# Attention with experts: the last two expert products of a batch move into head 0 of the attention

## The reference, cut to what matters

```
qkv = x @ W_qkv + b_qkv                       # 16 heads of 16 channels
attn = softmax(q k^T / 4);  attn_out = attn @ v
gate = softmax(x @ W_gate + b_gate)           # 8 experts
top_g, top_i = top_k(gate, 2);  combine = one_hot(top_i) weighted by top_g
expert_out = x @ W_experts[e] + b_experts[e]  # all 8 experts
moe_out = sum_e expert_out[e] * combine[e]
out = layernorm(x + attn_out + moe_out)
```

## Time and profile before

| | us |
|---|---|
| median of 3 runs | 3752.07 |
| lowest and highest | 3751.63, 3758.32 |
| the profiled execution | 3751.49 |
| its span in the trace | 3749.7 |
| mean granted clock of PE over the span | 0.973 of 2.4 GHz |

### The profile page before, as it was taken

How to read it: one execution, slowest core, us unless ns; L and a number is a source line. 1 busy time by engine, 2 the same in 40 slices (tenths; PEclk the granted TensorE clock), 3 DMA queues, 4 the chain that set the end, 5 groups by cost and what they waited for, 6 DMA issues and landing times.

```text
span 3749.7 us, 119956 instructions
## 1 busy us (share of the span) xinstructions
PE 3492.4 (93%) x52122; PEld 1583.7 (42%) x52122; DVE 3251.9 (87%) x3105; ACT 2589.8 (69%) x3896; POOL 1785.5 (48%) x1565
## 2 busy tenths in 40 slices
PE   5999999999999989998599999999999999999997
PEld 3655555454555545555332423324233242332422
DVE  5899989989999998998589797997979979799796
ACT  3665757666575766655269497695976959769598
POOL 4787878878887887888031210312103121031210
PEclk7999999999999999999799999999999999999999
DMA  3443545444453444444340602406024060240600
GB/s 95 132 121 105 149 109 137 115 132 124 109 152 100 136 121 126 125 106 115 91 69 2 102 13 42 73 2 93 22 39 76 2 94 21 39 76 2 91 13 13
DMA packets 145233, 307.78 MB, mean 82 GB/s; under 512 B 24484, under 2 KB 64068, under 8 KB 144452
## 3 DMA queue, kind: packets, MB, share of 16 engines
q1 hardware_dynamic: 144708, 300.10, 35.2%
HBM read 230.68 MB, written 35.13 MB: 71 GB/s over the span
## 4 chain that ended last, share of the span: by engine, by line
PE 22%; ACT 10%; DVE 10%; issue 9%; DMA 0%; SPq 0%; ACTq 0%; DVEq 0%; POOL 0%
ACT probs L1532 10%; PE ps L1332 7%; PE ps L1319 6%; DVE neg_max L1640 3%; PE ps L1367 2%; PE ps L1280 2%; PE ps L1442 2%; PE ps L1347 1%; PE ps L1380 1%; DVE acc L1774 1%; DVE acc L1763 1%; DVE att L1684 1%; DVE x1T L1622 1%; DVE x1T L1620 1%; DVE acc L1766 0%
## 5 line engine op out<-in xcount | busy, mean ns | idle before, releaser
L350 POOL TENSOR_TENSOR z<-z,c_rep 128x1024 f32<-128x1024 f32 x512 | 1412.8, 2770 | 330.9 <-DVE z L867 322.3
L1532 ACT ACTIVATE probs<-ps,e_scale 128x512 f32<-128x512 f32 x2048 | 1242.5, 696 | 118.2 <-PE ps L1319 117.8
L867 DVE TENSOR_TENSOR_SCAN z<-dA,ps 128x1024 f32<-128x1024 f32 x512 | 1157.8, 2278 | 130.2 <-PE ps L408 82.2
L1640 DVE TENSOR_REDUCE neg_max<-ps 128x1 f32<-128x1024 f32 x1024 | 1191.8, 1218 | 58.9 <-PE ps L1280 57.5
L708 ACT ACTIVATE dA<-rep,a_rep 128x1024 f32<-128x1024 f32 x512 | 565.4, 1142 | 217.9 <-DVE z L867 214.4
L408 PEld LDWEIGHTS ps<-diag,u_t 64*64 64x64 f32 x32768 | 531.9, 135 | 389.1 <-issue 388.7
L1319 PE MATMUL ps<-q_st,k_st 50*128 50x512 f16 x2048 | 648.9, 389 | 26.6 <-ACT probs L1532 20.1
L1332 PE MATMUL ps<-probs,v_h 128*32 128x256 f32 x8192 | 657.2, 395 | 0.6 <-ACT o_sb L1539 0.6
L408 PE MATMUL ps<-diag,u_t 64*64 64x64 f32 x32768 | 599.0, 222 | 59.7 <-DVE z L867 40.5
L1280 PE MATMUL ps<-k_st,q_st 48*128 48x512 f16 x2048 | 614.0, 388 | 7.5 <-DVE neg_max L1640 6.6
L427 PE MATMUL ps<-z,eye 128*64 128x512 f32 x2048 | 506.1, 615 | 2.8 <-POOL z L350 2.3
(11 more groups left out here) (189 smaller groups left out, 3107.2 us busy)
## 6 DMA issues: line engine op xcount, KB each, us to landing
c_rep<-c_scratch SPq DMA_DIRECT2D x512, 256.0 KB, 4.0
rep<-delta SPq DMA_DIRECT2D x128, 256.0 KB, 4.5
q_st<-qk_halves SPq DMA_DIRECT2D x192, 128.0 KB, 10.0
k_st<-qk_halves SPq DMA_DIRECT2D x192, 128.0 KB, 10.5
qk_halves<-qk_parts SPq DMA_DIRECT2D x32, 512.0 KB, 10.6
x_nat<-in_x SPq DMA_DIRECT2D x9, 1024.0 KB, 7.9
x_rows<-x_nat SPq DMA_DIRECT2D x9, 1024.0 KB, 6.8
xT<-in_xT SPq DMA_DIRECT2D x8, 1024.0 KB, 7.5
```

Of the source, the lines that this page charges most:

```text
L350: pool.tensor_tensor(z[:, k % ZR, :], z[:, k % ZR, :], c_rep[:, slot, :], ALU.mult).then_inc(s_zc, 1)
L867: dve.tensor_tensor_scan(z[:, k % ZR, :], dA[:, k % AR, :], pair(1 + k % 2), 0.0, ALU.mult, ALU.add).then_inc(s_z, 1)
L1532: act.activation(probs[:, kt, half * HALF:(half + 1) * HALF], ps[:, ring_bank(("probs", h, 2 * kt + half)), :], ACT.Exp, scale=e_scale[:, ...
L1640: dve.tensor_reduce(neg_max[:, h % 2, qt:qt + 1], pair(qt % 2), AX.X, ALU.max, negate=True).then_inc(s_mx, 1)
```

## The change

The products u = 30 and 31, both of tile 7, leave `experts` and are done in head 0: u = 30 after the two `scores_t` of turn 0 and u = 31 after those of turn 2, both into bank 6, which `weigh_v` first uses in turn 4. The helper functions `expert`, `scale_expert` and `add_scaled` hold what was written in the loops. DVE adds u = 30 after the first maximum of head 2 (`add_last_expert`), ACT scales u = 31 after the seventh exponential, and POOL adds it after the copies for head 0. `join(b, 7)` moves on DVE from behind the first maximum of head 2 to behind the seventh. The banks 4 and 5 are freed for head 0 by the products 27 and 28 instead of 30 and 31. `scaled` moves from `probs` to the first half of `sq_e`, a tile that is used only in the setup, and ACT's wait for POOL in turn 2 of head 0 goes away. SP's program is the same.

```diff
+        scaled = sq_e[:, 0:4, :].rearrange("p (s e) n -> p s e n", s=2)
-        scaled = probs[:, 2, :].rearrange("p (s e n) -> p s e n", s=2, e=2)
...
-        EBANK = tuple((u + 4) % 8 if u < 8 else 4 + u % 3 for u in range(EU))
+        LAST = EU - 2
+        EBANK = tuple((u + 4) % 8 if u < 8 else 4 + u % 3 if u < LAST else 6 for u in range(EU))
...
+                for i in range(LAST // 2):
+                    add_scaled(i)
...
                     take_v_head(h, 0, 5)
                     take_v_head(h, 5, TT)
+                    if h == 0:
+                        add_scaled(LAST // 2)
...
             def ring_free(b, user):
...
                 if n == -3:
-                    used(b, EU - 2)
+                    used(b, LAST - 3)
                 elif n == -2:
-                    used(b, EU - 1)
+                    used(b, LAST - 2)
...
             def weigh_v(b, h, kt):
...
+                if h == 0 and kt == 0:
+                    used(b, EU - 1)
...
             def step(b, h, before, ahead, front):
...
+                    if h == 0 and kt in (0, 2):
+                        expert(b, LAST + kt // 2)
...
             def exp_unit(b, h, kt, half):
...
-                if h == 0 and kt == 2:
-                    act.wait_ge(s_pa, (b + 1) * EU + 4)
...
+            def scale_expert(b, u):
+
+                i = u // 2
+                act.wait_ge(s_ex, b * EU + (u + 1))
+                act.wait_ge(s_pa, b * EU + (2 * i + 2))
...
+                mul.then_inc(s_ec, 1)
...
             def step(b, h, before, turned):
...
                         exp_unit(b, h, kt, half)
+                        if h == 0 and kt == 3 and half == 0:
+                            scale_expert(b, EU - 1)
...
+            def add_last_expert(b):
+
+                i = b * (EU // 2) + LAST // 2
+                t, e = LAST // (E // 2), 2 * (LAST % (E // 2))
+                bank = ps[:, EBANK[LAST], :]
+                dve.wait_ge(s_ex, b * EU + (LAST + 1))
+                dve.wait_ge(s_ea, i)
+                dve.scalar_tensor_tensor(out=acc[:, t, :], in0=bank[:, 0:H], scalar=comb_s[:, t, e:e + 1],
+                                         in1=acc[:, t, :], op0=ALU.mult, op1=ALU.add).then_inc(s_es, 1)
+                dve.wait_ge(s_es, i + 1)
+                dve.scalar_tensor_tensor(out=acc[:, t, :], in0=bank[:, H:2 * H], scalar=comb_s[:, t, e + 1:e + 2],
+                                         in1=acc[:, t, :], op0=ALU.mult, op1=ALU.add).then_inc(s_ea, 1)
...
             def step(b, h, before):
...
                     take_max(b, h + PRE, qt)
                     if qt == 0 and not before:
+                        add_last_expert(b)
+                    if qt == 6 and not before:
                         join(b, TT - 1)
```

More of the change, by code:

```diff
@@ L1243, in _, with add_scaled @@
             for b in range(NB):
-                for i in range(EU // 2):
+                def add_scaled(i):
                     to = x_in[:, i // 2, :]
@@ L1425, in used, with expert @@
                 pe.wait_ge(s_ec if u % 2 else s_ea, b * (EU // 2) + (u // 2 + 1))
+            def expert(b, u):
+                t, e2 = u // (E // 2), u % (E // 2)
+                if EPREV[u] is not None:
+                    used(b, EPREV[u])
+                for i, (k, w, x) in enumerate(TERMS):
+                    mm = pe.matmul(ps[:, EBANK[u], :], x1T[:, x, k, t * P:(t + 1) * P],
+                                   w_e[:, w, k, e2 * 2 * H:(e2 + 1) * 2 * H], start=(i == 0), stop=(i == len(TERMS) - 1))
+                mm.then_inc(s_ex, 1)
             def experts(b):
@@ L1432, in experts @@
                         u = t * (E // 2) + e2
-                        if EPREV[u] is not None:
-                            used(b, EPREV[u])
+                        if u >= LAST:
+                            break
                         if u == 3:
@@ L1440, in experts @@
                             pe.wait_ge(s_we, 2 * e2 + 2)
[L1441 to L1444, removed]
+                        expert(b, u)
                         if u in EARLY:
@@ L1545, in take_max @@
                 act.activation(m_rows[:, :], ps[0:2 * TT, ring_bank(("rows", h, 0)), 0:P], ACT.Copy).then_inc(s_mr, 1)
+            def scale_expert(b, u):
+                i = u // 2
+                act.wait_ge(s_ex, b * EU + (u + 1))
+                act.wait_ge(s_pa, b * EU + (2 * i + 2))
+                for e in range(2):
+                    mul = act.activation(scaled[:, i % 2, e, :], ps[:, EBANK[u], e * H:(e + 1) * H], ACT.Copy,
+                                         scale=comb_s[:, u // 4, 2 * (u % 4) + e:2 * (u % 4) + e + 1])
+                mul.then_inc(s_ec, 1)
             def step(b, h, before, turned):
@@ L1584, in experts @@
                 act.wait_ge(s_cbs, b + 1)
[L1585 to L1592, removed]
+                for u in range(1, LAST, 2):
+                    scale_expert(b, u)
                     if u == 7:
```

## The result

| | before | changed |
|---|---|---|
| median of 5 runs, us | 3751.63 | 3796.0 |
| lowest and highest | 3749.89, 3758.32 | 3790.59, 3801.64 |
| span of the profiled execution | 3749.7 | 3794.2 |

The ratio is 1.0117, with a 95% interval of 1.0102 to 1.0131: slower by 1.2%. 3786 was forecast, with 3768 to 3800 as the range.

The account below looks back on a forecast made before the run. No single engine was taken to bound the changed stage; PE, DVE and ACT hand over by turns. Late rows +21, half clock +13, eighth batch -0.9, summed as +33.5 on 3751.5 plus 0.6: 3786 us, range 3768 to 3800.

Parts of the forecast that it names:

- The late `join` holding SP's queue: Last join behind six more maxima, SP's load behind it, head 1's rows behind the load: +21 us in all.
- The time of the load: Second batch: load of x_in issued at 2167.05 instead of 2159.82, 7.2 us later.
- The additional waits in head 0: Between DVE's six maxima of head 2: 0.4 us for the fourth's scores, 0.8 for the fifth's.
- The landing behind the load: Head 1's row copies arrive only with the load ahead of them, so PE starts head 1 at 2172.25.
- X + 5.2: X is the load's issue; upper bound for the rows' arrival, taking the load's 5.2 us.
- the rival of the passing rows: Head 1's rows pass the load, X + 4.25 or sooner: 3779 or 3776 us; chance 0.12.
- My reason for the bound: The 1024 KB load, 0.4 us ahead, occupies all DMA engines nearly the whole time; copies are 1 KB each.
- The clock behind the stall: After PE's 5.6 us standstill, head 1 starts at half clock: 1.9 us a batch, times seven, +13 us.
- the forecast's own range: 3774 to 3797: clock term between 7 x 1.3 - 1 and 7 x 2.5, join 0.7 us sooner or later.
- the faster rival: Load and rows arrive in time for head 1, so head 0's gains stand: 15 us, 3737; chance 0.06.
- The gain in head 0: Earlier banks: head 0 alone shorter by 2.4 us in second batch, 0.9 in fifth and eighth; clock expected at 1.00.

Follow-up runs that it names:

- Experiments 1 and 3: 1: changed kernel, SP issues head 1's row copies before join wait and load, 3731.26 us; 3: kernel before, last join behind head 2's seventh maximum, 3804.48 us.
- Experiment 2: Changed kernel, with SP issuing head 1's row copies behind its wait for the joins but ahead of the load: 3776.85 us, ratio 1.0069.
- Experiment 9: Changed kernel, with four extra 128-row matmuls per batch among the experts, behind the scores that follow u = 18: 3797.87 us, ratio 1.0113.
- experiment 5: Kernel before, with one extra 128-row, 512-column matmul behind each of head 0's first four turns, result unread: 3732.7 us, ratio 0.9948.

## Why the prediction was right

**The late `join` holding SP's queue: right.** Experiments 1 and 3 show it from both sides: with SP's order mended the loss is gone, and with the `join` alone moved it is there.

**The time of the load: right.** 11.8 us from the end of u = 28's addition was worked out and 11.45 measured. The additional waits in head 0 were put at 0.4 and 0.8 us and are 0.20 and 1.03.

**The landing behind the load: right in kind, too small.** I took X + 5.2; in the second batch head 1 started at X + 5.74 (2173.63 - 2167.89), and over the seven it was X + 5.74 to X + 6.20, 5.96 in the mean. The longest was the third, whose load left at 2409.94:

```profile
2416.14 0.60 PE L1325 MATMUL ps<-q_st,k_st 50*128 50x512 f16 x1 [6.22 <-DMA q_st<-m_rows]
```

Experiment 2 shows that the place behind the load costs the copies 1.8 us, so the rival of the passing rows fell. My reason for the bound, that the load occupies the DMA engines for nearly the whole time, was too strong. In the second batch they are busy for 3.4 us, from 1.1 us behind the load's issue on, and then nearly idle for 1.2 us until PE starts:

```profile
2169.00:2172.40 3.40, 0.00 (x0) 0.00 (x0) 0.00 (x0) 0.00 (x0) 0.80 (x4) 0.63 0.91 305
2172.40:2173.60 1.20, 0.00 (x0) 0.00 (x0) 0.00 (x0) 0.00 (x0) 0.00 (x0) 0.50 0.04 9
```

The Trainium skill says in "DMA: Bandwidth & Descriptors", section "Queues, rings and completion order", that each DMA engine takes descriptors in ring order, and these times fit that. The same section says that a later descriptor may finish its write before an earlier one, so the rule gives an order of starting and no landing time; the prediction drew more from it than it holds. Whether the copies are late by that order or because they share the busy engines with the load, no run separates.

**The clock behind the stall: right in kind, too small.** It was put at 1.9 us for each batch. From 2173.63 to about 2180.1 head 1 ran at half clock, 6.5 us, of which 37% is 2.4 us.

**No half clock among the experts: the term that was missing.** In before one batch had it behind u = 18. In the changed kernel seven have it, right behind PE's pause of 1.92 us there, and each costs 1.4 us (experiment 2). The pause and what follows, in the changed kernel:

```profile
2135.18 4.45 PE L1443 MATMUL ps<-w_e,x1T 128*128 128x512 f16 x12 [1.92 <-DVE acc L1812]
```

Experiment 9 puts work of 128 rows in that pause, and the spell is gone, but this doesn't show that the pause makes it. The first experiment has the same pause in the same batch, with the same code there, and no spell:

```profile
2125.00:2145.00 20.00, 17.98 (x89) 7.02 (x88) 19.61 (x33) 11.77 (x26) 9.01 (x16) 1.00 0.93 107
...
2135.05 2.76 PE L1444 MATMUL ps<-w_e,x1T 128*128 128x512 f16 x12 [1.91 <-DVE acc L1813]
```

PE is busy for 17.98 of 20 us in this window, as in that of the changed kernel in experiment 9. Why the spell comes in seven batches of the one and in none of the other is not settled. The distance from one batch to the next differs between the kernels, and that is the only difference I know of there; experiment 9 changes that distance too.

**All together.** Two neighbouring loads are (3137.18 - 2167.89) / 4 = 242.3 us apart after and (3099.36 - 2159.82) / 4 = 234.9 before, so 7.4 us for each batch, where my terms gave 4.9:

```profile
3137.18 0.38 SPq L1140 DMA_DIRECT2D x_in<-x_rows  x1
```

From the end of u = 28's second addition to the start of head 1 it was 13.9 us before and is 17.4 now, in the mean of seven batches. These are 3.5 of the 7.4 us, where I had 3.0. The half clock in head 1 is 2.4 instead of 1.9, and that among the experts 1.2, less what before had of it, instead of nothing. 0.3 us are left open. Seven times 7.4 is 52 us. The eighth batch and the state-space stage, which was some 6 us shorter in this execution by the luck of the run, bring it to the 44.5 of the two spans.

So the range held, and partly by luck. The missing term alone is some 8 us. Two of the five executions, of 3801.60 and 3801.64 us, lie above the 3800 at which the range ended. Small slips in the working changed nothing: the printed terms add up to 33.1 and not 33.5, the ends of the forecast's own range come out at 3776 and 3795, and the faster rival takes 2.2 us where 2.4 had been worked out.

**The gain in head 0: right in size, wrong in reason.** I gave it to the earlier start and hoped for the clock beside it. In the first experiment head 1 started 11.4 us after the end of u = 28's second addition, as was worked out (2166.6 - 2155.25). But experiment 5 has the whole gain without the earlier start. DVE's rows there show the 1.54 us of waiting as before, and the moved work (two additions, a scaling, 12 matmuls) is not in head 0 either. So the moved work takes up what the earlier start gives, and what is gained is the clock. This is read from the two traces and the equal times; no run has the earlier start without the work. With four matmuls instead of the change, before gets the gain without any risk for SP's queue. That the moved products don't hold the clock in every case, experiment 9 shows.

## What to carry to other kernels

Before an instruction is moved later, look up who waits for its semaphore, and then everything that stands behind that waiter in its queue; here a 0.4 us addition was the gate of a DMA queue, and what was late was not the load that waited for it but the 1 KB copies behind. Put small, urgent copies ahead of waits and of large loads: here that turned 1.2% slower into 0.5% faster. Where a window of the profile shows half clock behind a stretch of narrow matmuls, try a few full ones whose result is thrown away before rearranging the program.

## What the runs showed of the hardware

- Four matmuls of 128 rows and 512 columns for each batch, of use to nobody, made the kernel 0.5% faster; the same four with 48 rows did nothing (0.9993).
- Four small copies took 3.50 us from the first issue until PE used their data, and 5.31 us with a 1 MB load issued 0.4 us ahead of them.
- Pauses of PE of 2.9 to 3.5 us before head 1 (experiment 2) were followed by half clock in all seven batches, as pauses of 5.8 to 6.2 us were in the changed kernel.
- A pause of 1.9 us among the experts was followed by 3.4 us of half clock in seven batches of the changed kernel and in none of the first experiment, with the same code there. So one profile of one kernel doesn't tell whether a stretch keeps its clock.
